# Four graph layers over 128 graphs: the order of work in the last eight slots, and where VectorE takes o out of PSUM

## What is computed

```
f0: A = adj @ x;  max over features of relu(A - A_own + A_own + b)
f1: h = x @ W; e = leaky_relu(s1[:, None] + s2[None, :]) * adj
    elu(softmax(e) @ h + beta * h)
f2: (adj @ x) @ weight + bias
f3: q, k, v = x @ Wq + bq, x @ Wk + bk, x @ Wv + bv   (8 heads of 64)
    softmax(q @ k.T / 8, masked where adj == 0) @ v
```

## Time and profile before

| | |
|---|---|
| median of three runs | 2518.2 us |
| profiled execution | 2518.76 us |
| its span in the trace | 2516.5 us |
| TensorE busy | 2434.1 us, 97% of the span |
| VectorE busy | 2207.9 us, 88% |
| slot 127 ends, slot 128 begins (TensorE) | 2385.24 us |
| slots 128 to 135 | 131.3 us |

### The profile page before, as it was taken

How to read it: one execution, slowest core, us unless ns; L and a number is a source line. 1 busy time by engine, 2 the same in 40 slices (tenths; PEclk the granted TensorE clock), 3 DMA queues, 4 the chain that set the end, 5 groups by cost and what they waited for, 6 DMA issues and landing times. The chain is left out here.

```text
span 2516.5 us, 54890 instructions
## 1 busy us (share of the span) xinstructions
PE 2434.1 (97%) x15501; PEld 2067.7 (82%) x15501; DVE 2207.9 (88%) x6954; ACT 1326.9 (53%) x4096; POOL 1444.3 (57%) x1793
## 2 busy tenths in 40 slices
PE   4899999999999999999999999999999999999985
PEld 3688888888888888888888888888888888888874
DVE  6799999999998998998998988988988988998863
ACT  3355555555555555555555555555555555555532
POOL 2465665655655665656656656556656656656531
PEclk9999999999999999999999999999999999999997
DMA  4256666666666566566566566666566666666554
GB/s 131 64 134 140 141 141 139 138 143 140 135 143 144 131 142 146 130 142 146 130 142 145 133 142 142 137 142 141 138 142 139 139 141 139 139 140 139 128 113 100
DMA packets 1375067, 340.98 MB, mean 135 GB/s; under 512 B 1078576, under 2 KB 1339312, under 8 KB 1375024
## 3 DMA queue, kind: packets, MB, share of 16 engines
q1 hardware_dynamic: 1375024, 340.47, 59.4%
HBM read 173.35 MB, written 166.99 MB: 135 GB/s over the span
## 5 line engine op out<-in xcount | busy, mean ns | idle before, releaser
L1796 PE MATMUL rot<-w_hi,y_hi 128*128 128x512 f32 x1024 | 415.6, 406 | 4.7 <-DVE y_lo L1708 3.4
L1798 PE MATMUL rot<-w_hi,y_lo 128*128 128x512 f32 x1024 | 403.8, 394 | 0.0
L1797 PE MATMUL rot<-w_lo,y_hi 128*128 128x512 f32 x1024 | 402.2, 393 | 0.0
L756 ACT ACTIVATE probs<-score,sc_nmax 128x128 f32<-128x128 f32 x1024 | 362.3, 370 | 42.0 <-DVE sc_nmax L1132 39.0
L482 POOL TENSOR_TENSOR ve<-mv,eps_col 128x1 f32<-128x1 f32 (+1 forms) x448 | 128.0, 286 | 389.4 <-DVE mv L1117 291.1
L590 POOL TENSOR_TENSOR x2b<-x,bias 128x512 f32<-128x512 f32 x120 | 156.0, 1300 | 242.9 <-DVE x L1450 242.9
L1132 DVE CUSTOM_DVE_ANT_0 score<-score,mask 128x128 f32<-128x128 f32 x1024 | 259.4, 315 | 0.0
L490 POOL TENSOR_TENSOR rs<-ve,half_neg 128x1 f32<-128x1 f32 (+1 forms) x448 | 252.7, 578 | 1.0
L1796 PEld LDWEIGHTS rot<-w_hi,y_hi 128*128 128x128 f32 x1024 | 194.0, 189 | 54.7 <-DVE y_lo L1708 3.9
L1151 DVE CUSTOM_DVE_ANT_0 dot_tmp<-x,u 128x512 bf16<-128x512 f32 x256 | 233.1, 946 | 4.9 <-ACT x L869 0.4
L600 POOL TENSOR_SCALAR e<-e 128x512 f32<-128x512 f32 x120 | 230.7, 1923 | 0.0
(11 more groups left out here) (242 smaller groups left out, 6920.0 us busy)
## 6 DMA issues: line engine op xcount, KB each, us to landing
pt_hbm<-probs SPq DMA_DIRECT2D x508, 128.0 KB, 2.8
probs_t<-pt_hbm SPq DMA_DIRECT2D x127, 512.0 KB, 4.0
x_in<-in_x SPq DMA_DIRECT2D x128, 256.0 KB, 4.1
xt_hbm<-x_b SPq DMA_DIRECT2D x512, 64.0 KB, 2.4
xt_f<-xt_hbm SPq DMA_DIRECT2D x128, 256.0 KB, 2.8
out_x<-x SPq DMA_DIRECT2D x128, 256.0 KB, 2.5
ot_hbm<-o_t SPq DMA_DIRECT2D x508, 64.0 KB, 1.9
o_norm<-ot_hbm SPq DMA_DIRECT2D x127, 256.0 KB, 2.7
```

The source lines that it names most:

```text
L756: ins = act.activation(probs[:, 0, c, t, :], score_tile(c, g, h), ACT.Exp, bias=sc_nmax[:, c, t:t + 1], scale=-1.0, accum_out=sc_sum[:, pa ...
L1796: pe.matmul(outp, lh, rh, start=first, stop=False)
L1797: pe.matmul(outp, lh, rl, start=False, stop=False)
L1798: return pe.matmul(outp, ll, rh, start=False, stop=last)
```

## The change

Only `drain` changes; instructions, shapes and buffers stay, apart from their order. `slot.drains()` is true in slots 128 to 135.

VectorE: y1_lo comes behind the dot products and the leaky relu of `L_ATT`; the copies of the last probabilities come behind y1_lo; taking o out of rot[3], as transposition or as the last copy, moves from ahead of the late joins to behind `masked_minimum(0)`:

```
                 statistics("3", x4[:, first + g, :], g)
-            if slot.on(L_PV):
-                slot.wait(dve, pv_mm, L_PV)
-                slot.wait(dve, ot_scattered, L_PV, 1, SCATTER)
-                (last_o_copied copy or o_t transposition)
             if slot.last(L_QK - 1):  join_parts(late_q), join_parts(late_k)
             if slot.on(L_GAT):  r1
             if slot.on(L_GCN):  y2_lo
             if slot.on(L_ATT):  att_inv, att_n
             if slot.on(L_QK):   masked_minimum(0)
+            if slot.on(L_PV):
+                (the same waits, copy or transposition)
             if last:  aggregate("3", 0, GROUP)
             if slot.on(L_QK):   masked_minimum(1)
```

TensorE: one chunk of k is projected between the two of q:

```
-    projection(q_bank, "wq", slot).then_inc(q_mm, 1)
+    if slot.drains():
+        projection(q_bank, "wq", slot, chunks=(0,))
+        slot.wait_last(pe, (y2_lo_done, L_GCN, 1), (k_done, L_QK, 1))
+        projection(k_bank, "wk", slot, chunks=(0,))
+        projection(q_bank, "wq", slot, chunks=(1,)).then_inc(q_mm, 1)
+    else:
+        projection(q_bank, "wq", slot).then_inc(q_mm, 1)
...
-    projection(k_bank, "wk", slot).then_inc(k_mm, 1)
+    projection(k_bank, "wk", slot, chunks=(1,) if slot.drains() else range(CHUNKS)).then_inc(k_mm, 1)
```

More of the change, by code:

```diff
@@ L727, in drain @@
                     low_x(Slot(slot.base, slot.offset + 1))
+                if slot.on(L_GCN):
+                    power(slot, "2", L_GCN)
             slots(pool, fill, emit, drain)
@@ L1038, in drain @@
                     late_parts(late_k, late_k_bank, kb_col).then_inc(k_part_done, 1)
+                if slot.on(L_GCN):
+                    slot.wait(act, z2_mm, L_GCN, 1)
+                    slot.wait(act, y2_mm, L_GCN)
+                    act.activation(y2_hi[:, :], rot[2][:, :], ACT.Copy).then_inc(y2_hi_done, 1)
                 if slot.on(L_QK):
@@ L1061, in drain @@
                                    scale=rs["0"][:, e2, 0:1]).then_inc(x1_done, 1)
+                if slot.on(L_QK):
+                    exponentials(slot, 1).then_inc(score_exp, 1)
+                if slot.after().on(L_EDGE) and not slot.after().fills():
+                    round_x(Slot(slot.base, slot.offset + 1))
                 if slot.on(L_ATT):
@@ L1622, in drain @@
                     statistics("0", x_in[:, e4, :])
+                if slot.on(L_GAT):
+                    slot.wait(dve, y1_hi_done, L_GAT)
+                    dve.tensor_tensor(y1_lo[:, :], rot[1][:, :], y1_hi[:, :].bitcast(F32), ALU.subtract)\
+                        .then_inc(y1_lo_done, 1)
+                if slot.last(L_PV):
+                    for h, bank in enumerate((rot[1], s2_bank)):
+                        dve.wait_ge(last_pt_mm, h + 1)
+                        dve.tensor_copy(probs_t[:, :, h:TILES:2, :],
+                                        bank[:, :].rearrange("p (c g n) -> p c g n", c=CHUNKS, g=GROUP))\
+                           .then_inc(last_pt_done, 1)
                 if slot.on(L_GCN):
@@ L1746, in drain @@
                                       ALU.mult, ALU.mult).then_inc(edge_b_done, 1)
+                if slot.on(L_PV):
+                    slot.wait(dve, pv_mm, L_PV)
+                    slot.wait(dve, ot_scattered, L_PV, 1, SCATTER)
+                    if slot.last(L_PV):
+                        dve.tensor_copy(o_t[:, :], rot[3][:, :]).then_inc(last_o_copied, 1)
+                    else:
+                        dve.transpose(o_t[:, :], rot[3][:, :]).then_inc(o_t_done, 1)
                 if last:
@@ L1839, in _, with projection @@
             y2 = [a[:, :].rearrange("p (k n) -> p k n", k=KC) for a in (y2_hi, y2_lo)]
-            def projection(banks, w, slot, late=False):
+            def projection(banks, w, slot, late=False, chunks=range(CHUNKS)):
                 w_hi, w_lo = weights[w]
                 first = slot.buf(L_QK, BUFS) // GROUP * GROUP
-                for c, bank in enumerate(banks):
-                    chunk = slot.part(L_QK) * CHUNKS + c
+                for c in chunks:
+                    bank, chunk = banks[c], slot.part(L_QK) * CHUNKS + c
                     cols = slice(chunk * P, (chunk + 1) * P)
```

60 lines of the change are left out of this document (23 added, 37 removed).

## The result

| | before | after |
|---|---|---|
| median, 7 runs each | 2518.22 us | 2509.72 us |
| lowest and highest | 2517.70, 2524.41 | 2507.95, 2513.37 |
| profiled execution, its span | 2518.76, 2516.5 us | 2511.4, 2509.6 us |
| slot 128 begins (TensorE) | 2385.24 | 2387.08 |
| from there to the end | 131.26 us | 122.52 us |

The ratio of the times is 0.996, interval 0.995 to 0.997: 8.5 us faster, 0.9 beyond the 7.6 that can be told from no change. 2509.5 had been predicted. The two profiled spans differ by only 6.9 us, because this execution of the kernel after came 1.84 us later into slot 128, over instructions that are the same in both.

The account below looks back on a forecast made before the run. TensorE's own work was taken to bound the loop; only 131.3 us in the last eight slots, where it waits, could move. Gains less contention sum to 8.65 us: 2510.1 against the profiled execution, 2509.5 against the median; range 2506.8 to 2515.6.

Parts of the forecast that it names:

- slot 128: Gap ahead of att_n's transposition and slow z2 go, partly taken back by y1_lo and att_t: 2.6 us gained.
- slot 129: z2's wait for y2_lo, which stood behind o_t and r1, goes: 2.0 us gained, at least 1.0.
- slot 130: z2's same wait, o_t's 0.64 and y2_lo's 0.7, goes: 1.4 us gained, at least 0.64.
- slot 131: z2 has run out and v still waits for o_t, which starts as before: no gain counted.
- slot 132, up to the late parts of k: Start of slot 132, before k's late parts: no gain counted.
- late parts to the transposition of the probabilities: In slot 132 the minima no longer stand behind o_t, so exponentials end sooner: 1.9 us gained, ends 1.0 and 2.0.
- from there to slot 133's PV (contention): SP's transfers come closer together and take longer: 0.5 us taken off, ends 0 and 1.5.
- slot 133's PV to the last copy: First minima and exponentials finish before PV, then o_norm limits: 1.1 us gained, ends 0.6 and 1.3.
- last copy to the end: In slots 134 and 135 GpSimd's add_eps goes ahead of neg_mean: 0.15 us gained.
- the signs that were to show the forecast wrong: Growing PV wait in slots 130 to 133, scatter to gather over 5 us, or new 0.63 us matmuls.
- The first rival: Transfers become each slot's chain once TensorE stops waiting for VectorE; 3.65 us left, 2514.6; chance 0.18.
- The slower rival: Moved waits leave slot 132's four projections at the low clock, costing 11.2 us: 2520.7; chance 0.06.

Follow-up runs that it names:

- second execution: The changed kernel with no line changed, profiled once more: 2511.7 us, ratio 0.9974; 122.66 us from slot 128 to the end.
- only-o_t kernel: The kernel before with one edit, VectorE's o_t (with the last copy) behind the first minima: 2510.13 us, ratio 0.9968.
- o_t-back kernel: The changed kernel with o_t and the last copy back ahead of the late joins: 2519.2 us, ratio 0.9993.
- chunk back: The changed kernel with q and k projected whole, one after the other, in the drain: 2509.81 us, ratio 0.996.
- att_t ahead: The changed kernel with ScalarE's att_t ahead of xt_hi and the exponentials of h = 1: 2511.77 us, ratio 0.9965.
- xt_hi late: The changed kernel with ScalarE's xt_hi behind the exponentials of h = 1: 2511.26 us, ratio 0.9966.
- late gather: The changed kernel with SP's gather of slot 132's o behind the scatter of slot 133's probabilities: 2511.86 us, ratio 0.996.
- GpSimd's order back: The changed kernel with layer 2's power ahead of layer 1's and neg_mean ahead of add_eps: 2512.01 us, ratio 0.9968.

## Why the prediction was right

The terms of the sum, in us, by distances in the two traces:

| term | predicted | measured | with the second execution |
|---|---|---|---|
| slot 128 | 2.6 | 2.59 | 3.57 |
| slot 129 | 2.0 | 1.87 | 1.94 |
| slot 130 | 1.4 | 0.81 | 1.80 |
| slot 131 | 0 | 1.46 | -0.90 |
| slot 132, up to the late parts of k | 0 | -0.13 | 0.03 |
| late parts to the transposition of the probabilities | 1.9 | 2.07 | 2.06 |
| from there to slot 133's PV (contention) | -0.5 | -1.20 | -1.07 |
| slot 133's PV to the last copy | 1.1 | 1.12 | 1.05 |
| last copy to the end | 0.15 | 0.15 | 0.12 |
| sum | 8.65 | 8.74 | 8.60 |

The main mechanism was right: what TensorE waited for stood behind o_t, and the waits named went. The two executions also tell which terms are firm. Slot 129 and all from slot 132 on agree within 0.16; in slots 128, 130 and 131 the single terms move by 1.0 to 2.4. That slot 128 came out at 2.59 is luck, then, and so is how well the errors cancel.

*Slot 128* was read rightly in its parts. The gap ahead of att_n's transposition and the slow z2 went together, as the only-o_t kernel (18.06, that is 4.75 less, where 4.6 was said for the two) and the o_t-back kernel (23.31) show. What took part back were z1's wait for y1_lo (0.28, where 0.45 was said) and the wait for att_t (1.37, and 0.38 in the second execution), which came by ScalarE waiting for xt_f ahead of xt_hi. Another 0.5 in both is assigned to neither. Both next-in-line waits were shown by experiment: with the chunk back the first was gone, with att_t ahead or xt_hi late the second.

*Slots 129 and 130.* z2's brackets went as predicted. In slot 130 0.6 is missing in the first trace: from 2432.9 to 2436.4 the clock was at 0.60, and the scores took 2.08 instead of 1.16. The wait of 1.81 ahead is the same in the kernel before, at a clock of 1.00, so it alone doesn't explain it. The second execution kept 1.00 and gave 1.80: z2's 1.39, and 0.35 less of waiting for PV's transfer (0.49 for 0.84).

*Slot 131* was put at nothing and gave 1.46, for the clock stayed at 1.00 there. This isn't the change's doing in any firm sense: the same program had 0.81 in another execution, and was 0.90 slower there than before. So the close sum holds errors that nearly cancel, +1.46 here against 0.59 in slot 130 and 0.70 at the contention, and in the second execution +0.97 in slot 128 and +0.40 in slot 130 against 0.90 here and 0.57.

*Contention* was under-sized: -0.5 against -1.20. The nearest row was rightly named (o's gather just ahead of slot 133's scatter), and the late gather shows its price, 1.1. The upper end of 1.5 was kept in the range. Of the signs that were to show the forecast wrong, three are there beside its right number: scatter to gather over 5 us in slot 133 (5.48), PV waits that grew (0.65 to 0.93 in slot 132, none to 0.15 in slot 131), and slow matmuls in slot 130 where there were none. They show where its sizes were off, not that the waits behind o_t were misread.

*The first rival*, the transfers as the chain, had a chance of 0.18 and was counted as an alternative to the forecast. A part of it came in beside it. The only-o_t kernel is 2.16 shorter in slot 128 and takes the same 122.52 (to the hundredth by chance); three other kernels with slot 128 at 18.7 take 122.45, 123.75 and 124.89. In three traces slot 132 waits for xt_lo (0.99, 0.76, and 0.47 with k's chunk back), and there the transfers decide. In the others slot 131 is long by PV's wait and a low clock; that the one brings the other isn't shown, and the kernel before has the low clock there without that wait. The argument against the rival, that SP idles over 5 us for o_t in slots 132 and 133, looked at the wrong slots: the chain shown is tight in 130 and 131.

*The slower rival's* mechanism was seen in size but not in place. Slot 131 took up to 3.3 more where its clock was low (15.46 and 18.77), 2.4 more within one program. Slot 132's projections it never reached: their first 11.2 us ran at 0.96 to 1.00 in all thirteen traces.

*What the forecast did not say* is that four of the five edits together give nothing but the 0.12 of add_eps. It had costed them one by one at nothing or small losses, which was right, and wrote one sum; that they cost 1.2 to 2.2 in slot 128 and nothing that can be told at the end could be seen only with the edits apart. VectorE's move of y1_lo and of the last probabilities' copies, and ScalarE's moves of y2_hi and of the late q parts, were undone only together with the others, not each alone.

What stays open: why the executions with att_t ahead, GpSimd's order back and the late gather (twice) begin slot 132 1.8 to 2.7 later than the change. In each of them slot 131 ran at 0.73 to 0.81, but so it did (0.81) in the two that began slot 132 at 71.32 and 72.00.

## What to carry to other kernels

Where a matmul engine waits for a vector engine, look what the vector engine did first when it was woken: a copy that only frees a bank may stand behind everything that someone waits for, if that bank is needed late. Undo the edits of a bundle and also do the strongest alone; here one of five carried all but 0.12 us. Profile one program twice before reading a slot's difference: here single slots moved by up to 2.4 us with no line changed. Once an order is repaired, a saving further ahead may not reach the end (0.5 to 2.2 us in slot 128 never did here), so look at where the following stage's input lands before working on the present one.

## What the runs showed of the chip

*The clock fell behind waits, but no one wait tells when.* In slot 131 TensorE waits 2.38 for the join of q, and then in most traces for PV's transfer. Where the second wait was 0.15 or 0.18 the slot's clock was 1.00 and 0.90; where it was 0.55, 0.58, 0.71, 1.25, 1.28, 1.31 and 1.45 it was 0.75, 0.73, 0.73, 0.81, 0.75, 0.81 and 0.81. With the first wait filled down to 0.55 it was 1.00, 0.90 and 0.81 with second waits of 1.07, 1.02 and 1.41. And the kernel before, with the 2.38 and no second wait at all, was at 0.80; its scores and PV there took 1.50 and 1.97 instead of 1.16 and 1.09:

```profile
2454.91 1.50 PE L2169 MATMUL score<-k_sb,q_sb 64*128 64x128 f32 x16 [2.38 <-DVE q_sb L1140]
...
2456.55 1.97 PE L2207 MATMUL rot<-probs_t,v_sb 128*64 128x128 f32 x16
```

That is thirteen single traces and no rule. In slot 130 a wait of 1.81 (once 2.69) stands in all thirteen. In four of them the slot's clock was 0.90 or 0.91, in the other nine, the kernel before and the second execution of the change among them, 1.00. In the change's first trace it was 0.60 just behind that wait:

```profile
2432.90:2436.40 3.50, 3.42 (x26) 3.00 (x26) 1.29 (x3) 0.60 (x1) 0.59 (x1) 0.60 0.91 209
```

*The first slots differ from execution to execution.* The instructions up to slot 128 are the same in all kernels here, and yet slot 128 began anywhere from 2383.28 to 2390.47. The windows from 60 to 100 us show where it arises, first before, then after, then the kernel with the late gather (slot 128 at 2385.24, 2387.08 and 2389.20):

```profile
60.00:80.00 20.00, 14.35 (x60) 10.69 (x61) 17.40 (x44) 4.57 (x11) 9.97 (x13) 0.91 0.18 43
80.00:100.00 20.00, 17.67 (x98) 14.59 (x96) 14.48 (x35) 6.54 (x15) 8.54 (x11) 1.00 0.16 40
```

```profile
60.00:80.00 20.00, 14.85 (x53) 11.07 (x54) 16.05 (x41) 4.15 (x10) 9.21 (x12) 0.79 0.16 39
80.00:100.00 20.00, 17.70 (x89) 14.48 (x89) 13.66 (x34) 6.09 (x14) 8.71 (x11) 0.95 0.16 41
```

```profile
60.00:80.00 20.00, 14.37 (x49) 10.26 (x50) 15.45 (x42) 4.40 (x10) 7.43 (x10) 0.76 0.16 39
80.00:100.00 20.00, 17.61 (x85) 14.32 (x84) 14.24 (x34) 5.26 (x12) 8.71 (x10) 0.90 0.17 41
```

TensorE is busy for 14.35, 14.85 and 14.37 us of the first 20, at clocks of 0.91, 0.79 and 0.76, and got through 60, 53 and 49 pieces of its work (the number in brackets). One and the same slot begins at 204.78, 206.75 and 208.90 in the three, 1.97 and 4.12 apart from the first, and slot 128 still 1.84 and 3.96. From 200 to 2385 us TensorE is busy for 2184.7 to 2184.8 of 2185 us in each, so what is lost at the start isn't made up. Why the clock differs there stays open. An edit's 1 or 2 us can't be read from one whole time against such a spread of up to 7 us. From the slots it touches it can be read only as far as two executions of one program agree: here within 0.14 us from slot 128 to the end, but only within 1.0 in slots 128 and 130 and 2.4 in slot 131.
